# Router logits from rows not yet normalised, contexts turned once and keys moved, in a two-layer gated attention and expert kernel

## The reference, cut to what matters

```
x = x + tanh(g_xattn[0]) * ln(x) * scan(0.9, ctx*ctx)            # retention, quadratic in the context
x = x + tanh(g_ffn[0])   * moe0(ln(x))        # softmax over ln(x) @ Wg, two best, capacity 640, W_in, gelu(a)*g, W_out
q, k, v = ln(x) @ Wq.T + bq, ctx @ Wk.T + bk, ctx @ Wv.T + bv
x = x + tanh(g_xattn[1]) * softmax(q @ k.T / 16 + masks) @ v     # per batch
x = x + tanh(g_ffn[1])   * moe1(ln(x))        # two best of ln(x) @ gate_w.T, softmax of the two, w1, silu, w2
```

## Time and profile before

| | us |
|---|---|
| median of 3 runs | 644.23 (641.95 to 648.24) |
| the profiled execution | 645.89 |
| its span, first to last instruction | 644.0 |

### The profile page before, as it was taken

The page is one execution under the profiler, slowest core; times in us unless marked ns, Lnnn a source line. Parts: engine busy times, 40 slices in busy tenths (PEclk is TensorE's granted clock), DMA queues, the critical chain, the costliest instruction groups (busy, mean ns, idle before and its releaser), DMA issues.

```text
span 644.0 us, 12062 instructions
## 1 busy us (share of the span) xinstructions
PE 552.7 (86%) x3567; PEld 491.3 (76%) x3568; DVE 329.6 (51%) x812; ACT 323.0 (50%) x646; POOL 229.5 (36%) x258
## 2 busy tenths in 40 slices
PE   4897868799999989897776439999999999999991
PEld 2466558799999889865666328898989889889881
DVE  2574826266556635264864673455453544453530
ACT  3493435166466636337675223456454555544530
POOL 3300174154554503347000013354454445354441
PEclk9896679699999979989796558999999999999997
DMA  8923052234444323352024005344452445253221
GB/s 277 373 82 130 10 171 58 94 94 167 161 132 151 105 92 136 109 171 91 33 67 163 1 18 157 98 106 106 106 159 45 120 106 151 39 163 48 34 40 21
DMA packets 51091, 70.59 MB, mean 110 GB/s; under 512 B 6832, under 2 KB 42928, under 8 KB 51056
## 3 DMA queue, kind: packets, MB, share of 16 engines
q1 hardware_dynamic: 40352, 50.04, 23.7%
q0 software_dynamic: 10704, 20.10, 14.4%
HBM read 49.80 MB, written 20.33 MB: 109 GB/s over the span
## 4 chain that ended last, share of the span: by engine, by line
PE 68%; DVE 12%; issue 7%; ACT 5%; DMA 3%; POOL 1%; SPq 1%; DVEq 1%; POOLq 0%; ACTq 0%
PE PA L1413 23%; PE PD L1413 19%; PE PC L1413 8%; PE PC L1282 4%; PE PC L1575 3%; PE PD L1282 3%; PE PB L1276 2%; PE PA L1282 2%; DVE ys L990 1%; DVE wlo L1096 1%; ACT xn L587 1%; PE PB L1425 1%; DVE stats L860 1%; DMA xg<-xn_rows,row_x 1%; PE PB L1557 1%
## 5 line engine op out<-in xcount | busy, mean ns | idle before, releaser
L1413 PE MATMUL PD<-whi,hhi 128*128 128x256 f32 x420 | 123.3, 294 | 0.0
L1413 PE MATMUL PD<-wlo,hhi 128*128 128x256 f32 x420 | 119.3, 284 | 0.0
L1413 PE MATMUL PD<-whi,hlo 128*128 128x256 f32 x420 | 119.3, 284 | 0.0
L541 POOL DMA_INDIRECT out<-ys,row_o x35 | 55.8, 1595 | 105.3 <-DVE ys L1233 105.0
L1413 PEld LDWEIGHTS PD<-wlo,hhi 128*128 128x128 f32 x420 | 80.9, 193 | 0.0
L1413 PEld LDWEIGHTS PD<-whi,hlo 128*128 128x128 f32 x420 | 80.8, 192 | 0.0
L1413 PEld LDWEIGHTS PD<-whi,hhi 128*128 128x128 f32 x420 | 80.7, 192 | 0.1
L818 ACT ACTIVATE hhi<-PC 128x512 fp32r<-128x512 f32 x70 | 38.0, 595 | 67.7 <-PE PC L1575 67.7
L521 POOL DMA_INDIRECT xg<-xn_rows,row_x x38 | 39.3, 1035 | 89.9 <-DVEq L974 72.3
L466 POOL DMA_INDIRECT xg<-xn_rows,row_x x40 | 41.0, 1024 | 80.0 <-DVEq L974 46.6
L473 POOL DMA_INDIRECT y_rows<-ys,row_y x40 | 42.1, 1054 | 75.9 <-ACT ys L677 70.2
(11 more groups left out here) (233 smaller groups left out, 1307.2 us busy)
## 6 DMA issues: line engine op xcount, KB each, us to landing
raw<-w SPq DMA_DIRECT2D x16, 1024.0 KB
raw<-L_ffn_W_in SPq DMA_DIRECT2D x8, 1024.0 KB
raw<-L_ffn_W_out SPq DMA_DIRECT2D x8, 512.0 KB
y_rows<-ys SPq DMA_DIRECT2D x8, 512.0 KB, 8.3
xn_rows<-xn SPq DMA_DIRECT2D x8, 512.0 KB, 3.5
xs<-x SPq DMA_DIRECT2D x4, 512.0 KB, 6.5
cx<-ctx SPq DMA_DIRECT2D x4, 512.0 KB, 6.9
ys<-y_rows SPq DMA_DIRECT2D x4, 512.0 KB, 4.4
```

Source lines behind the costliest of these rows:

```text
L541: pool.indirect_dma_start(out, bass.IndirectOffsetOnAxis(ap=row_o[:, j:j + 1], axis=0), ys[:, j % 2, :], None, compute_op=ALU.add).then_in ...
L1413: mm = pe.matmul(dst, a[k], b[k], start=(first and k == 0 and a is lhs_hi and b is rhs_hi), stop=(last and k == n - 1 and a is lhs_lo))
```

## The change

Router logits are made from rows that are not yet normalised. The router weights are centred first: a product of `ones` with `wg` in `weights` gives their column sums, `wg_mean` is that over -256, and VectorE adds it to `wg` (the row's mean then drops out of the product). The two best are taken from these logits; the root of the token is multiplied in only where gates are made. So in layer 0 `rows(q)` turns `xs` as soon as the retention is added (`x1_ready`), and normalise(1, q) only feeds `xn_rows`.

In layer 1 the logits of a quad are the sum of two products. The router of the old rows, before attention, runs on the `xT` that the scores use, directly behind them, and is multiplied by the old root (`sd`). The probabilities times `vg` (values times router weights, made from the context by `value_gates` with `wvg`, the product of Wv and the router weights, 24 columns) stand before the value product, and are multiplied by the factor of the attention. `mixed_logits` adds both. The turns and routers of norm 3 and their copies go away. `attended(3)` and coefs(3, 3) move behind one_hots(1) and pick; the gates of layer 1 are made and written in one piece, behind the third of four map parts.

Contexts are turned once. Quads 0 and 1 are turned into the places of `gT` that quads 3 and 2 get later; keys(1), biases(1), values(1) stand between the map of layer 0 and the first expert; quad 2 is turned, with keys, biases, values and value gates, before the loop of the third stage; quad 3 inside it, behind the scores and the router of quad 0. `gates0` and `pad(0)` stand before the first split of expert 0's rows. One more small vector (bv by columns) is loaded ahead of quad 1 of `x`, Wv by rows ahead of the mask, and POOL spreads two more columns.

The diff, cut to its core:

```diff
+        def context_at(q):
+            if q < 2:
+                return gT[:, :, (NQ - 1 - q) * QN:(NQ - q) * QN]
+            return flat(xn[:, 1]).rearrange("p (c n) -> p c n", c=DC)
...
+        EV1 = {at: k + 1 for k, at in enumerate((
+            ("cT", 0), ("w", 0), ("xT", 0), ("gT", 0), ("wv", 0), ("xT", 1), ("cT", 1), ("xT", 2), ("xT", 3),
+            ("v", 0), ("bias", 0), ("gT", 1), ("bias", 1), ("v", 1),
+            ("cT", 2), ("gT", 2), ("bias", 2), ("v", 2),
+            ("cT", 3), ("gT", 3), ("bias", 3), ("v", 3)))}
...
+                act.activation(flat(wg_mean[:, :, :]), wg_sum, ACT.Copy, scale=-1.0 / D).then_inc(evac_done, 1)
...
+            root(0, 0)
+            normalise(0, 0, xn0[0])
+            root(0, 1)
+            normalise(0, 1, xn0[1])
+            context_out(0)
+            root(1, 0)
+            root(0, 2)
+            normalise1(0)
+            normalise(0, 2, xn0[0])
+            weights_out()
+            rows_out(0)
+            root(1, 1)
+            root(0, 3)
+            normalise1(1)
+            normalise(0, 3, xn0[1])
+            keys_out(0)
+            value_weights_out()
+            rows_out(1)
+            root(1, 2)
+            context_out(1)
+            normalise1(2)
+            rows_out(2)
+            root(1, 3)
+            rows_out(3)
+            normalise1(3)
...
-            context_out("cT again", 0)
             for k in range(DC):
                 win0(0, k)
-            for k in range(2):
-                wout0(0, k)
             part_part(0)
+            values_out(0)
             biases_out(0)
             act.wait_ge(e_arg, 1)
             act.activation(lg[:, :, :], lg[:, :, :], ACT.Exp)
             act.activation(rr[:, 1, :], rr[:, 0, :], ACT.Exp).then_inc(e_ready, 1)
-            values_out(0)
+            for k in range(2):
+                wout0(0, k)
+            keys_out(1)
+            biases_out(1)
+            values_out(1)
...
-            context_out("cT again", 1)
+            def context_rest(q):
+                keys_out(q)
+                biases_out(q)
+                values_out(q)
+
+            context_out(2)
             split1(win_in[1], 16, win_hi[1], piece_in)
-            values_out(1)
-            biases_out(1)
-            context_out("cT again", 2)
-            values_out(2)
-            biases_out(2)
-            context_out("cT again", 3)
+            context_rest(2)
...
+                if t == 0:
+                    context_out(3)
+                    context_rest(3)
...
+                    dve.sem_inc(x1_ready, 1)
...
+                    dve.wait_ge(evac_done, EV1["w", 0])
+                    link(dve.tensor_tensor(wg[:, :, :, :], wg[:, :, :, :],
+                                           wg_mean[:, :, :].unsqueeze(2).broadcast_to([P, 2, DC, E]), ALU.add))
+                    dve.sem_inc(wg_ready, 1)
+                if t == 3:
+                    choose(0)
+                if t == NQ:
+                    choose(1)
+                    choose(2)
+            choose(NQ - 1)
+
+            def gate_diff():
+                link(dve.tensor_tensor(rr[:, 0, :], top[:, :, 1], top[:, :, 0], ALU.subtract))
+                link(dve.tensor_tensor(rr[:, 0, :], rr[:, 0, :], root_of(3), ALU.mult))
...
                         .then_inc(map_ready, 1)
+                    if layer == 1 and n == 2:
+                        gate_values()
...
+            of_token = root_of(1)
+            link(dve.tensor_tensor(lg[:, :, :], lg[:, :, :], of_token.unsqueeze(2).broadcast_to([P, NB, E]), ALU.mult))
             link(dve.tensor_tensor(rr[:, 0, :], top[:, :, 1], top[:, :, 0], ALU.subtract))
+            link(dve.tensor_tensor(rr[:, 0, :], rr[:, 0, :], of_token, ALU.mult))
...
+            def value_gates(q):
+
+                dve.wait_ge(vg_done, q + 1)
+                link(dve.tensor_tensor(vg[:, q * QB:(q + 1) * QB, :], vg_at(q).rearrange("p (b e) -> p b e", e=E),
+                                       wvg[:, DC:DC + 1, :].broadcast_to([P, QB, E]), ALU.add))
+                dve.sem_inc(vg_ready, 1)
...
+            value_gates(0)
+            gates0()
             for k in range(2):
                 wout0(0, k)
+            dve.wait_ge(mask_in, 16)
+            pad(0)
+            value_gates(1)
             for pair in range(PAIRS):
                 xt0(0, pair)
             hid0(0, first=True)
-            gates0()
-            dve.wait_ge(mask_in, 16)
-            pad(0)
...
+            def mixed_logits(q):
+
+                dve.wait_ge(lg_done, NQ + q + 1)
+                quad = slice(q * QB, (q + 1) * QB)
+                link(dve.tensor_tensor(lg[:, quad, :], logits[:, quad, :],
+                                       sd[:, place(2, q), :].unsqueeze(2).broadcast_to([P, QB, E]), ALU.mult))
+                link(dve.tensor_tensor(part_lg[:, :, :], mixed[:, quad, :],
+                                       att[:, q % 2, 3, :].unsqueeze(2).broadcast_to([P, QB, E]), ALU.mult))
+                dve.sem_inc(lg_used, 1)
+                link(dve.tensor_tensor(lg[:, quad, :], lg[:, quad, :], part_lg[:, :, :], ALU.add))
+
+            def attended(q):
+
+                dve.wait_ge(pv_done, q + 1)
+                for b in range(QB):
+                    xb = xs[:, q * QB + b, :]
+                    ins = dve.scalar_tensor_tensor(xb, PC[:, b // 2, (b % 2) * D:(b % 2 + 1) * D],
+                                                   att[:, q % 2, 3, b:b + 1], xb, ALU.mult, ALU.add)
+                link(ins)
+                dve.sem_inc(pv_used, 1)
+                norm_stats(3, q)
+
...
-                    dve.wait_ge(pv_done, q + 1)
...
-                    norm_stats(3, q)
-                for q in late(t):
-                    coefs(3, q)
+                    mixed_logits(q)
+                    if q < NQ - 1:
+                        attended(q)
+                    best_two(lg, range(q * QB, (q + 1) * QB))
+                if t == NQ:
...
-            for q in range(1, NQ - 1):
-                choose(1, q)
-            gate_diff(0, NQ - 1)
-            gate_values(0, 0, NQ - 1)
-            choose(1, NQ - 1)
             one_hots(1)
+            attended(NQ - 1)
...
+            coefs(3, NQ - 1)
+            gate_diff()
...
             def router(layer, q):
+                pe.wait_ge(wg_ready, 1)
                 if layer * NQ + q >= 1:
-                    pe.wait_ge(lg_used, layer * NQ + q)
+                    pe.wait_ge(lg_used, layer * NQ + (max(q - 1, 0) if layer else q))
                 for b in range(QB):
                     mm = product(PD[:, 0, (q * QB + b) * E:(q * QB + b + 1) * E],
                                  [xT[:, k, b * P:(b + 1) * P] for k in range(DC)],
                                  [wg[:, layer, k, :] for k in range(DC)])
-                mm.then_inc(lg_done, 1)
+                if layer == 0:
+                    mm.then_inc(lg_done, 1)
...
-            def context(n, q):
+            def value_weights():
+
+                pe.wait_ge(wv_in, 16)
+                pe.wait_ge(wg_ready, 1)
+                for k in range(DC):
+                    product(wvg_psum[:, k * E:(k + 1) * E], [wv_rows[:, m, k * P:(k + 1) * P] for m in range(DC)],
+                            [wg[:, 1, m, :] for m in range(DC)])
+                product(wvg_psum[:, DC * E:(DC + 1) * E], [bv_wide[:, m, :] for m in range(DC)],
+                        [wg[:, 1, m, :] for m in range(DC)]).then_inc(evac_ready, 1)
...
 
                 pe.wait_ge(ctx_in[q], 16)
-                if n == "cT" and q >= 1:
-                    pe.wait_ge(evac_done, EV1["xT", q - 3] if q >= 3 else EV1["cT", q - 1])
-                elif n == "cT again":
-                    pe.wait_ge(evac_done, EV1[n, q - 1] if q >= 1 else EV1[n, q] - 1)
+                pe.wait_ge(evac_done, EV1["cT", q] - 1)
                 turn(cx[:, q * QB:(q + 1) * QB, :]).then_inc(evac_ready, 1)
 
+            def rows(q):
+
+                pe.wait_ge(x1_ready, q + 1)
+                pe.wait_ge(evac_done, EV1[(("cT", 0), ("xT", 0), ("cT", 1), ("xT", 2))[q]])
+                turn(xs[:, q * QB:(q + 1) * QB, :]).then_inc(evac_ready, 1)
...
 
-            for t in range(NQ + 2):
-                if t < NQ:
-                    context("cT", t)
-                    retention(t)
-                if t == 0:
-                    weights()
-                if t >= 2:
-                    q = t - 2
-                    pe.wait_ge(xn_ready, XN[1, q])
-                    if t < NQ:
-                        pe.wait_ge(evac_done, EV1["cT", t])
-                    else:
-                        pe.wait_ge(evac_done, EV1["xT", q - 1])
-                    turn(xn[:, q % 2]).then_inc(evac_ready, 1)
-                if t < NQ:
-                    keys(t)
-                if t >= 2:
-                    pe.wait_ge(evac_done, EV1["xT", t - 2])
-                    router(0, t - 2)
+            def rows_router(q):
+                pe.wait_ge(evac_done, EV1["xT", q])
```

(66 more changed lines are left out.)

206 lines of the change are left out of this document (90 added, 116 removed).

## The result

The changed kernel took 649.86 us (median of 5 runs, 647.68 to 650.95) beside 644.23 before: ratio 1.0075, 95% interval [1.0041, 1.0108]. The forecast was 641, 3 us under before. So the change costs some 5.5 us, just inside the range given (632 to 650), but on the other side of no change.

The account below looks back on a forecast made before the run. Expert layers were taken as bound by TensorE's own work, the two other stages by chains of waits between engines. A -3.5, B -3.8 and C +4.0 sum to -3.3 us: 641 against the median 644.23, range 632 to 650.

Parts of the forecast that it names:

- A: Stage before the first expert: earlier routing, partly spent on work moved behind the map; -3.5 us, ends +1 and -8.5.
- B: First expert: gates and mask of quad 0 moved to where VectorE waits anyway; -3.8 us, bounds 0 and -4.4.
- C: Stage between the expert layers: later normalise(2, 1), earlier routing and slow scores; +4.0 us, ends -2 and +8.
- The loop: Stage C, normalise(2, 1) to normalise(2, 3): first round bound by ScalarE, second by VectorE; 24.0 us against 22.0 before.
- Scores(3) to one-hots: Stage C, from the start of scores(3) to layer 1's one-hots: 15.1 us against 33.5 before.
- the map chain: Stage C, between one-hots and map: attended(3) adds 3.6 us, coefs and gate_diff 0.9.
- C, the clock: Stage C: scores(0), scores(1) and scores(3) start at half clock after waits, 2 us each; 4.2 of the possible 6 taken.
- -0.2: Stage C without the clock term: one-hots 4.7 us earlier, then 3.6 and 0.9 more ahead of the map.
- The fast start of expert 0: End of stage A: first twelve products may take 1.8 us instead of 3.56, and 0.3 less on the next twelve.
- rival 3: Moved work takes all of the earlier routing's gain (A 0), all three scores slow; +2.2, 648.1 or 646.4 us; chance 0.16.

Follow-up runs that it names:

- quad3_ahead: Changed kernel with quad 3's turn, keys, biases, values and value gates ahead of the third stage's loop, directly behind quad 2's; 0.9888 of the kernel before.
- quad3_again: The kernel of quad3_ahead timed once more, with more rounds; 0.9904 of the kernel before.
- bias_last: Changed kernel with GpSimd's shares of quads 2 and 3 ahead of value_bias(3) in its queue; 1.0117 of the kernel before.
- warm: The kernel of fill plus two idle products of 320 columns behind each turn, where TensorE waits for the copy; 0.9983 of the kernel before.
- norm_first: Changed kernel with ScalarE's root and normalisation of quad 1 ahead of the copies of quad 3's keys, biases and values; 0.9985 of the kernel before.
- gates_b: Kernel before with only gates0 and pad(0) moved as in the change, ahead of expert 0's first splits; 0.9977 of the kernel before.
- late_quad1: Changed kernel with quad 1's keys, biases, values and value gates behind the first expert layer; 1.0293 of the kernel before.
- old_gates: Changed kernel with gates0 and pad(0) back behind the first hidden rows of expert 0; 1.0125 of the kernel before.
- before_shift: Kernel before with 16 products of 8 columns at TensorE's start, shifting its later code; 0.9983 of the kernel before.
- after_shift16: Changed kernel with 16 products of 8 columns at TensorE's start; 1.0097 of the kernel before.
- keys1_gap: quad3_ahead with keys(1) behind layer 0's last router and VectorE's value_gates(0) ahead of its splits of expert 0's weights; 0.9875 of the kernel before.
- keys1_early: Changed kernel with keys(1) between the turn and the router of quad 2 on TensorE; 1.0109 of the kernel before.
- fill: Changed kernel with three idle products of 512 columns ahead of the turns of quads 0, 1 and 3; 1.0115 of the kernel before.

## Why the prediction was wrong

The sum was A -3.5, B -3.8, C +4.0. Measured it is A +2.7, B between -0.8 and -2.1, C +8.8, and two things that stood in no step: -5.7 by the exit stall and +0.6 to +0.9 in the last stage. Two steps failed, C and A, and a third was too large. That 649.86 still lies inside the range of 632 to 650 is luck: without the 5.7 us, which no step had, it would lie outside.

**C, the waits (forecast +4.0, measured +8.8).** The place of the price was right: normalise(2, 1) was forecast 11.8 us later, and moving quad 3's group takes 10.4 us of C away in quad3_ahead, 9.7 in quad3_again. The size was not. Normalise(2, 1) came 15.0 us later: 1.3 by the slow scores(0), 1.8 by VectorE's four-column product beside value_bias(3), a neighbour that the forecast did not give it. The loop took 25.5 us instead of 24.0. I had left GpSimd's queue out, where the shares of quads 2 and 3 wait behind value_bias(3); but bias_last shows that this lengthens the combination and not the stage. Scores(3) to one-hots took 19.3 instead of 15.1, the map chain 4.65 more than before, as forecast (4.5).

**C, the clock.** I took 4.2 us beside a sum of -0.2. warm gives back 3.4 net of its fillers, so this term about held; but -0.2 was too low by 5.6. In warm, 2.8 of these lie ahead of normalise(2, 1) (with keys(3) at half clock, 5.40 us), 1.8 in the loop. The rule named with the forecast (the Trainium skill, TensorE: Matmul & The Clock Gate, HAM oscillation) said that all three scores start slow. The trace of after agrees, with 1.22 us for the first four each time; but in quad3_again three quads of four began at full clock, one of them behind a wait of 1.11 us, so it is no rule for every execution here.

**A (forecast -3.5, measured +2.7).** Map, moved work and its length were right: 84.0 for its end in the profiled after against 83.2. Two things were not. The one-hots came on average at 59.7 (eleven executions, 57.39 to 61.26) and not at 56.6. The forecast let VectorE hold the chain there and took the products of the value weights as hidden. In the traces TensorE holds it without a gap from router(0, 0) to context(1): keys(0) take 5.1 to 6.5 us instead of 3.5, and the value weights 1.24 that were put at nothing; behind them the copy for router(0, 2) waits some 0.7 us for normalise(1, 2) on ScalarE. And from one-hots to first product it is 30.5 to 33.2 us, depending on whether keys(1) starts slow (5.38 instead of 3.68 in norm_first) or TensorE stalls 2.5 us ahead of the first turn (quad3_again); 29.5 were forecast (86.1 less 56.6). The fast start of expert 0, which the -3.5 also counted on, did not come: the granted clock was 0.50 from 88 to 94. The ten executions with after's first stage give 91.2 on average, before's two (before, gates_b) 88.6; with so wide a spread the 2.7 us are good to one or two. This is rival 3 for A, and 2.7 us worse. late_quad1 shows that quad 1's group does it.

**B (forecast -3.8).** Up to the entry of the loop, expert 0's products took 3.1 us less in after (25.4 instead of 28.5) and 4.2 in gates_b, near the forecast. The sentence that failed is "The stall behind it, where the program enters its loop with no work pending anywhere, stays." It grew by 1.9 in after against old_gates and by 2.1 in gates_b. Work ahead of it was made shorter and the stall took half or more of the gain.

**What was in no step.** The stall at the loop's exit, 3.90 us and 2.1 us of slow products behind it, is missing in after (0.30). before_shift loses it by 16 small products at the start, and after_shift16 and late_quad1 have one again (3.41, 5.08). So it comes and goes with the place of TensorE's code, and was a gift of 5.7 us; without it after would stand at 1.016 to 1.019 of before, by my estimate from these numbers. Why the exit of a loop stalls at one place and not at another was not tried, and the cause stays open.

**Where the gain of the change is.** With quad 3's group ahead of the loop it is 0.989 to 0.990 of before, by the experts' stretch (-6.0 to -9.2) and C (-1.0 to -1.7), while A costs 1.3 to 3.3. So most of the gain is the exit stall that the code's new place took away: without those 5.7 us the kernel would stand at about 0.998 of before, by the same estimate. The new router alone has not been shown to pay; quad3_ahead is the version to keep, and keys1_gap adds nothing to it that can be told.

## To carry over

A group of matmuls that is moved takes its copies with it: ask which small step of the elementwise engines (a root, a norm) stands behind these copies in its queue, and put the group so that the long chain is served first; here it was worth 10 us, or 1.6% of the whole. Moving that step alone brought about 1. A gap that is filled from one side is often only moved: four times in this study (keys1_early, bias_last, keys1_gap, B) the next wait in line took over what was removed, so forecast what is late next and at which clock. When a stretch that was hardly touched changes by several microseconds, look for idle time with nothing pending and shift the code before crediting the change.

## What the runs showed of the chip

- TensorE stalled 3.4 to 5.1 us at the exit of its loop in some kernels and 4.2 to 6.5 at the entry in all, with no semaphore pending. The exit stall depends on where the code lies: 16 small products at the start take it away in one kernel (before_shift) and bring one back in the other (after_shift16). The entry stall grows by some 2 us when the work ahead of it ends earlier (gates_b against before, after against old_gates).
- A VectorE product of 128 x 4 took 2.00 us beside GpSimd's addition of 128 x 1024, and 0.16 away from it; six combinations of 128 x 256 took 4.58 beside GpSimd's shares and 2.58 away from them.
- Idle products held the clock only if they stood in the last gap ahead of the group: ahead of the turn alone (fill) two groups of scores began at half clock and the third fell to it, behind the turn as well (warm) all ran at full clock.
- 64 products of 8 columns, each with its 128 x 128 weights loaded anew, took 27.3 us at the start, 0.43 each, at a granted clock of 1.00.
